# Graph attention layer, one core: the chunk end on VectorE and ScalarE, TensorE's program without loops, ScalarE's compares two steps ahead

## The reference

```python
# x: [8192, 128], adj: [8192, 8192] of 0 and 1, W: [128, 128], a_l, a_r: [4, 32]
mask = (adj + eye(8192)) > 0
Wh = (x @ W.T).reshape(8192, 4, 32)
l = einsum('nhd,hd->nh', Wh, a_l);  r = einsum('nhd,hd->nh', Wh, a_r)
e = l[:, :, None] + r.T[None, :, :]
e = where(e >= 0, e, 0.2 * e)
alpha = softmax(where(mask[:, None, :], e, -inf), axis=2)
out = elu(einsum('nhm,mhd->nhd', alpha, Wh).reshape(8192, 128))
y = layernorm(x + out)            # over the last axis, eps 1e-5
```

## Time and profile before

| | |
|---|---|
| median of 3 runs | 1956.38 us (1952.86 to 1957.16) |
| the profiled execution | 1956.05 us, span 1954.3 us |
| mean granted TensorE clock | 0.946 of 2.4 GHz |
| busy: TensorE matmul, VectorE, ScalarE, GpSimd | 86%, 95%, 87%, 12% |
| DMA | 418.06 MB, mean 214 GB/s |

### The profile page before, as it was taken

One profiled execution on the slowest core, in us unless ns is written; L12 is line 12 of the kernel. 1 busy time (PEld: TensorE's weight loads), 2 busy tenths in 40 slices (PEclk: granted clock), 3 DMA queues, 4 the chain that ended last, 5 costly groups with the idle time before them and its releaser, 6 DMA issues.

```text
span 1954.3 us, 83257 instructions
## 1 busy us (share of the span) xinstructions
PE 1676.7 (86%) x37063; PEld 1650.0 (84%) x37063; DVE 1850.1 (95%) x2056; ACT 1696.2 (87%) x1791; POOL 228.2 (12%) x106
## 2 busy tenths in 40 slices
PE   5188899798978999788988989889898889989894
PEld 5187799797978989788988989789897889989894
DVE  6699999999999999999999999999999999999995
ACT  3599899798988999798989989789897899979892
POOL 1000100401022010211004010220102110040103
PEclk8599999999999999999999999899998999999997
DMA  7899576676666767666766767567675657665221
GB/s 230 313 328 341 194 257 225 202 228 229 209 200 218 255 210 238 202 212 211 236 220 207 236 220 232 193 205 255 207 236 181 227 190 255 230 200 170 60 68 28
DMA packets 240287, 418.06 MB, mean 214 GB/s; under 512 B 14400, under 2 KB 104896, under 8 KB 238016
## 3 DMA queue, kind: packets, MB, share of 16 engines
q1 hardware_dynamic: 240064, 414.83, 64.6%
HBM read 397.48 MB, written 17.30 MB: 212 GB/s over the span
## 4 chain that ended last, share of the span: by engine, by line
ACT 44%; DVE 22%; PE 18%; issue 9%; DMA 5%; POOL 1%; SPq 0%; DVEq 0%; ACTq 0%; POOLq 0%
ACT bmask L446 40%; PE psum L335 15%; DVE bmask L591 7%; DVE bmask L603 5%; DVE cmask L609 5%; ACT acache L414 3%; DMA abuf<-in_adj_dram 3%; DVE acc L615 2%; DMA vring<-v_scratch 2%; PE trp L315 1%; PE psum L280 1%; DMA v_scratch<-vt 1%; DVE st L657 1%; PE psum L289 0%; DVE acache L539 0%
## 5 line engine op out<-in xcount | busy, mean ns | idle before, releaser
L446 ACT ACTIVATE bmask<-lrow,rtab 128x1024 fp8e4<-128x1024 f32 x1450 | 1540.7, 1149 | 11.5 <-PE psum L335 11.5
L335 PE MATMUL psum<-vring,bmask 128*128 128x99 bf16 x16384 | 843.0, 210 | 96.1 <-DVE bmask L603 48.1
L335 PE MATMUL psum<-vring,cmask 128*128 128x99 bf16 x16384 | 844.6, 211 | 89.1 <-DVE cmask L609 80.4
L335 PEld LDWEIGHTS psum<-vring,bmask 128*128 128x128 fp8e4 x16384 | 780.5, 99 | 107.8 <-issue 99.0
L335 PEld LDWEIGHTS psum<-vring,cmask 128*128 128x128 fp8e4 x16384 | 778.5, 99 | 100.5 <-issue 83.4
L603 DVE TENSOR_TENSOR bmask<-bmask,acache 128x1024 int32<-128x1024 int32 x512 | 632.2, 1235 | 41.3 <-ACT bmask L446 32.3
L609 DVE TENSOR_TENSOR cmask<-acache,bmask 128x1024 int32<-128x1024 int32 x512 | 654.7, 1279 | 11.8 <-PE psum L335 11.7
L591 DVE TENSOR_SCALAR bmask<-lrow,rtab 128x1024 fp8e4<-128x1024 f32 x598 | 500.0, 848 | 0.0
L414 ACT CAST acache<-trp 128x512 int32<-128x512 f32 x256 | 148.5, 580 | 167.3 <-PE trp L315 167.0
L720 POOL TENSOR_TENSOR late<-acc,wgt 128x1024 f32<-128x1024 f32 x16 | 45.0, 2810 | 1493.8 <-DVE wgt L645 1493.8
L315 PE MATMUL trp<-pack,abuf 128*128 128x32 bf16 x4096 | 144.1, 177 | 53.7 <-ACT acache L414 32.0
(11 more groups left out here) (60 smaller groups left out, 258.5 us busy)
## 6 DMA issues: line engine op xcount, KB each, us to landing
abuf<-in_adj_dram SPq DMA_DIRECT2D x256, 1024.0 KB, 8.0
vring<-v_scratch SPq DMA_DIRECT2D x512, 198.0 KB, 3.4
lrow<-l_scratch SPq DMA_DIRECT2D x16, 1024.0 KB, 10.8
v_scratch<-vt SPq DMA_DIRECT2D x16, 792.0 KB, 9.5
bmask<-in_x_dram SPq DMA_DIRECT2D x16, 256.0 KB, 2.9
late<-in_x_dram SPq DMA_DIRECT2D x32, 128.0 KB, 4.8
out_dram<-late SPq DMA_DIRECT2D x32, 128.0 KB, 6.1
l_scratch<-cmask SPq DMA_DIRECT2D x1, 128.0 KB, 3.7
```

The costliest lines, as they stand in the source:

```text
L335: return nc.tensor.matmul(psum[:, bank, at * S3:(at + 1) * S3], mask[:, i, j * P:(j + 1) * P], vring[:, slot, i, col:col + S3], start=open ...
L446: last = nc.scalar.activation(bmask[:, q % 4, h, i], lrow[:, p, h], ACT.Relu, bias=rtab[:, t, H + hh:H + hh + 1], scale=BIG, saturate=False)
```

## The change

- GpSimd's `weigh_sums`, `residual` and `normalise` go. It keeps two operations of 128x8 per chunk: variance + eps and the power.
- VectorE takes the multiplication by the weights in step 2 (128x1024), the sum of the branches and the minimum (128x512 each) in step 3. Once per chunk it makes `zz` = max(value, 0) + x in one operation in step 5 and adds exp - 1 in step 6 (before: 9). The statistics are in step 7 (before: 10), and `mean_part` (128x8) in step 9.
- ScalarE takes the exponential in step 4 (before: 6), and the normalisation itself: eight activations of 128x128 with a scale and a bias per row, two in each of the steps 11 to 14. The result lies in `em` and no longer in `pm`.
- ScalarE's iteration q now does compare(q + 2), and then the same evacuation. VectorE's compares stay one step ahead.
- TensorE's program is written out for all 512 steps: no loops, no registers, no `settle`. Its matmuls and their order are the same.

```diff
--- before.py
+++ after.py
@@ -109,7 +109,7 @@
         pm = late[:, 0:ITEMS * DK].rearrange("p (i d) -> p i d", d=DK)
         ov, mn, em, zz, xr = (late[:, ITEMS * DK + i * SUB * D:ITEMS * DK + (i + 1) * SUB * D].rearrange("p (j d) -> p j d", d=D)
                               for i in range(5))
-        yout = pm.rearrange("p i d -> p (i d)").rearrange("p (j d) -> p j d", d=D)
+        yout = em
         VF = G * 2 * HP * E
         WB = NT * HP * E
         whole = acache.rearrange("p t n -> p (t n)").bitcast(fp32)
...
@@ -204,14 +197,14 @@
                 return rows[c * CI:(c + 1) * CI, :].rearrange("(j s w) d -> s w j d", s=4, w=P // 4)[s]
 
             def load_xr(c):
-                wait(sp, y_ready, c)
+                wait(sp, z_done, c)
                 if c == 0:
                     sp.wait_ge(v_lo, NP * NG)
                 for s in range(4):
                     sp.dma_start(xr[s::4], as_bytes(x, c, s)).then_inc(xr_in, 16)
 
             def store_y(c):
-                sp.wait_ge(y_ready, c + 1)
+                sp.wait_ge(y_ready, SUB * (c + 1))
                 for s in range(4):
                     sp.dma_start(as_bytes(out, c, s), yout[s::4]).then_inc(y_stored, 16)
 
...
@@ -300,98 +290,55 @@
                 last = nc.tensor.transpose(psum[:, BANKS - 2, a * P:(a + 1) * P], l_t[:, a], identf[:, :])
             last.then_inc(l_back, 1)
 
-            def turn_pair(base, m, u):
-
-                buf = m // 2 % 2
-                if m % 2 == 0:
-                    pe.wait_ge(a_loaded[buf], 8 * base + 32 * u + 32 * (m // 4) + 32)
-                wait(pe, evac_done, base + m + 4 * u)
-                if not (isinstance(base, int) and isinstance(u, int)):
-                    settle()
+            def turn_pair(r):
+
+                buf = r // 2 % 2
+                if r % 2 == 0:
+                    pe.wait_ge(a_loaded[buf], 32 * (r // 4 + 1))
+                wait(pe, evac_done, r)
                 for i in range(2):
-                    at = (2 * m + i) % JB
+                    at = (2 * r + i) % JB
                     for j in range(SUB):
                         block_hi = abuf[:, buf, j, at * P:(at + 1) * P].bitcast(bf16)[:, 1::2]
                         last = nc.tensor.matmul(trp[:, i, j * P // 4:(j + 1) * P // 4], block_hi, pack[:, :], start=True, stop=True)
                 last.then_inc(tr_done, 1)
 
-            def step(c, p, u, k, first=False, turned=None):
-
-                slot, cslot = k % 4, k % 2
-                q = (c * NP + p) * STEPS + 8 * u + k
+            def step(q):
+                c, p, s = WHERE[q]
                 w = c * NP + p
-
-                def opens(bank):
-                    wait(pe, bank_free, BANKS * (w - 1) + bank + 1)
-                    if not isinstance(c, int):
-                        settle()
 
                 def product(mask, item, i, h, b, j):
                     bank, at = item // PB, item % PB
-                    opening = first and i == 0 and at == 0
+                    opening = s == 0 and i == 0 and at == 0
                     if opening:
-                        opens(bank)
+                        wait(pe, bank_free, BANKS * (w - 1) + bank + 1)
                     col = (h * 2 + b) * S3
                     return nc.tensor.matmul(psum[:, bank, at * S3:(at + 1) * S3], mask[:, i, j * P:(j + 1) * P],
-                                            vring[:, slot, i, col:col + S3], start=opening, stop=True, skip_group_check=True)
-
-                pe.wait_ge(v_in[slot], 16 * ((c * NP + p) * (STEPS // 4) + 2 * u + k // 4 + 1))
+                                            vring[:, q % 4, i, col:col + S3], start=opening, stop=True, skip_group_check=True)
+
+                pe.wait_ge(v_in[q % 4], 16 * (q // 4 + 1))
                 pe.wait_ge(b_ready, q + 1)
-                if not isinstance(q, int):
-                    settle()
                 for i in range(2):
                     for h in range(HP):
                         for j in range(SUB):
-                            last = product(bmask[:, slot, h], h * SUB + j, i, h, 0, j)
+                            last = product(bmask[:, q % 4, h], h * SUB + j, i, h, 0, j)
                 last.then_inc(half_done, 1)
-                if turned:
-                    turn_pair(*turned)
+                for r in TURNED[q]:
+                    turn_pair(r)
                 pe.wait_ge(c_ready, q + 1)
-                if not isinstance(q, int):
-                    settle()
                 for i in range(2):
                     for h in range(HP):
                         for j in range(SUB):
-                            last = product(cmask[:, cslot, h], (HP + h) * SUB + j, i, h, 1, j)
+                            last = product(cmask[:, q % 2, h], (HP + h) * SUB + j, i, h, 1, j)
                 last.then_inc(mm_done, 1)
...
-            def one_pass(c, p):
-
-                base = c * STEPS + p * STEPS // 2 + LEAD - LEAD % 4
-                eight(c, p, 0, True, base, SECOND, 0)
-                with pe.Fori(1, 4) as u:
-                    eight(c, p, u, False, base, SECOND, u)
 
             pe.wait_ge(pack_made, 1)
             for r in range(AHEAD):
-                turn_pair(0, r, 0)
+                turn_pair(r)
...
-            with pe.Fori(1, NC - 1) as c:
-                one_pass(c, 0)
-                one_pass(c, 1)
...
+            for q in range(Q):
+                step(q)
 
 
         @block.scalar
...
@@ -448,19 +395,27 @@
                 last.then_inc(cmp_act, 1)
 
             def elu_exp(w):
-                p = w % NP
-                act.wait_ge(mn_ready, w + 1)
-                nc.scalar.activation(em[:, :, p * HP * DK:(p + 1) * HP * DK], mn[:, :, p * HP * DK:(p + 1) * HP * DK],
-                                     ACT.Exp).then_inc(em_ready, 1)
+                c, p = w // NP, w % NP
+                mine = slice(p * HP * DK, (p + 1) * HP * DK)
+                act.wait_ge(mn_done, w + 1)
+                wait(act, y_stored, 4 * 16 * c)
+                nc.scalar.activation(em[:, :, mine], mn[:, :, mine], ACT.Exp).then_inc(em_done, 1)
+
+            def normalise(c, subs):
+                act.wait_ge(nmr_done, c + 1)
+                for j in subs:
+                    nc.scalar.activation(yout[:, j], zz[:, j], ACT.Identity, bias=nmr[:, j:j + 1],
+                                         scale=vrs[:, j:j + 1]).then_inc(y_ready, 1)
 
             act.wait_ge(um_done, 1)
             for b in range(2):
                 nc.scalar.activation(uu[:, :, b], um[:, b], ACT.Exp).then_inc(uu_done, 1)
             compare(0)
+            compare(1)
             for q in range(Q):
                 c, p, s = WHERE[q]
-                if q + 1 < Q:
-                    compare(q + 1)
+                if q + 2 < Q:
+                    compare(q + 2)
                 if q > 0:
                     for n in TURNED[q - 1]:
                         evacuate(n)
...
@@ -468,9 +423,12 @@
                     highest(NG + s // EVERY_STEPS)
                 if q < STEPS and s % EVERY_STEPS == 3:
                     middle(NG + s // EVERY_STEPS)
-                if s == 6 and q > STEPS:
+                if s == 4 and q > STEPS:
                     elu_exp(c * NP + p - 1)
+                if c > 0 and p == 0 and s in (11, 12, 13, 14):
+                    normalise(c - 1, (2 * s - 22, 2 * s - 21))
             elu_exp(NC * NP - 1)
+            normalise(NC - 1, range(SUB))
 
 
         @block.vector
...
@@ -618,8 +576,6 @@
 
             def take_first_sums(w):
                 dve.wait_ge(half_done, STEPS * (w + 1))
-                if w > 0:
-                    dve.wait_ge(pool_step, POOL_STEPS * ((w - 1) // 2) + 1 + 2 * ((w - 1) % 2))
                 add_parts(range(FIRST_BANKS))
 
             def take_last_sums(w):
...
+            def weigh_sums(w):
+                dve.wait_ge(dn_step, 4 * w + 4)
+                nc.vector.tensor_tensor(pm[:, :], acc[:, :, 0:DK], wgt.rearrange("p (i o) -> p i o", o=1).to_broadcast([P, ITEMS, DK]),
+                                        ALU.mult).then_inc(pm_done, 1)
+
+            def add_halves(w):
+                p = w % NP
+                mine = slice(p * HP * DK, (p + 1) * HP * DK)
+                p2 = pm.rearrange("p (b h j) d -> p b h j d", h=HP, b=2)
+                dve.wait_ge(pm_done, w + 1)
+                nc.vector.tensor_tensor(ov[:, :, mine].rearrange("p j (h d) -> p h j d", h=HP), p2[:, 0], p2[:, 1],
+                                        ALU.add).then_inc(ov_done, 1)
+                dve.wait_ge(ov_done, w + 1)
+                nc.vector.tensor_scalar(mn[:, :, mine], ov[:, :, mine], 0.0, None, ALU.min).then_inc(mn_done, 1)
+
+            def residual(c):
+                dve.wait_ge(ov_done, NP * (c + 1))
+                dve.wait_ge(xr_in, 4 * 16 * (c + 1))
+                wait(dve, y_ready, SUB * c)
```

(51 more changed lines are left out.)

76 lines of the change are left out of this document (8 added, 68 removed).

## The result

The changed kernel takes **1859.58 us** (median of 4 runs, 1858.71 to 1860.64), beside 1956.77 us for the kernel before on the same chip: a ratio of 0.9508, 95% interval 0.9491 to 0.9524. That is 97 us less. The forecast was 74 less. The profiled execution took 1858.71 us, with a span of 1856.8.

What follows compares the result with a forecast made beforehand. Three engines were nearly level, with VectorE late at the chunk end, slowed by GpSimd. From 1956 us: -91 GpSimd's work, +42 VectorE's new work, -17 ScalarE's lead, 0 TensorE's program, -8 the end, giving 1882; own range 1870 to 1897, whole 1858 to 1912.

Steps and rivals of the forecast that it cites:

- part 2: VectorE's new chunk-end work (weights, sum, minimum, zz, mean_part), with no cover: +42 us, bounds 38 and 52.
- part 3: ScalarE's compares two steps ahead shorten VectorE's waits for ScalarE: -17 us, bounds 0 and -32.
- Part 1: GpSimd's chunk-end work goes, so VectorE's compares and masks beside it are no longer slowed: -91 us.
- The rule that a saturated VectorE may shed work: Rival: long VectorE compares have another cause than GpSimd, so lost time does not come back: 1990 us, chance 0.02.
- the 22 that I took: VectorE's waits for ScalarE: 22 of the 29.6 us taken back through ScalarE's longer lead.
- The 5 that I had given back: Deduction of 5 us from the lead's gain, for TensorE being late next and ScalarE's new activations.
- part 4: TensorE's program written out, the chunk loop's branch being covered at the pass border: 0 us, bounds -10 and +11.
- The ring: Limit on ScalarE's lead: compare(q + 2) waits until step q - 2 is through TensorE; no separate size.
- The gaps in the middle of groups: TensorE's issue gaps between matmuls, 10.8 us in 17 places; at most some 11 us more from fetching every step.
- Part 5: After the last pass, from the weights to the store: 19.3 us becomes 11.3, -8 us.
- the first: Rival: ScalarE's lead lasts and TensorE keeps up: 1867 us, or 1858 with cheap new VectorE work; chance 0.22.
- the third rival: TensorE is starved of instructions at packet borders, some 340 packets, 40 in a pair of passes: 1970 us, chance 0.04.

Runs made afterwards that it cites:

- a_poolop: Changed kernel plus one GpSimd operation of 128x1024 per pass on a tile of its own, needed by nobody: 1886.51 us, ratio 0.9671.
- a_loops: Changed kernel with the earlier kernel's TensorE block back (Fori loops, registers, settle): 1877.69 us, ratio 0.9615.
- a_ring5: Changed kernel with five slots in place of four for the masks of branch 0, compares waiting for a step one further back: 1853.42 us.
- b_straight: Kernel before with TensorE's program written out and nothing else: 1951.79 us beside 1950.86, ratio 1.0008.
- a_nolead: Changed kernel with ScalarE's compares one step ahead again in place of two: 1890.14 us, ratio 0.9681.

## Why the prediction was right, and where it was not

The direction was right and the time lies in the whole range, 1858 to 1912, but only just, and outside my own range, 1870 to 1897. That it lies inside is luck as well: the low edge does not follow from my bounds. 1867 with 38 in place of 42 for part 2 is 1863, not 1858, and 1859.58 is below it.

The windows place the 97.5 us by which the span is shorter:

| | us |
|---|---|
| VectorE's busy time, passes 1 to 15 | -65.0 |
| VectorE's idle time, passes 1 to 15 | -26.0 |
| before pass 1 | -1.5 |
| after pass 15 | -5.0 |

Parts 1 and 2 stood for the first line, with -49, part 3 for the second, with -17. By the terms of the sum:

- **Part 1, -91: the right mechanism, 8 us too small.** 99.3 us came back. I had taken L591's undisturbed time from its busy sum, 500.0 - 598 x 0.748. But busy is the time in which at least one is under way, and pairs of compares overlap. The mean is the right number: 598 x (0.848 - 0.748) = 59.8, not 52.7. a_poolop shows the cause by itself. The two small GpSimd operations were indeed free: L549's mean is 0.747. With 8 us more here, parts 1 and 2 would give -57; the other 8 of the -65.0 are in none of my terms, and no run says where they come from.
- **Part 2, +42: right.** 1.22, 0.68, 0.43 and 1.22 us measured, for 1.22, 0.68, 0.40 and 1.22 taken. The rule that a saturated VectorE may shed work, even to GpSimd (the Trainium skill, Perfetto Trace Analysis, Optimizing Scalar/DVE Operations), would have meant 1990 us. The run decides against it here: VectorE with more work is busy 60 us less. The same section's reservation, that moves between these two might not help because they share a port, agrees with a_poolop; that it is the port, no run here shows.
- **Part 3, -17: too small.** VectorE's idle time in passes 1 to 14 fell by 25.3 us (39.9 to 14.6). Its waits for ScalarE fell by 21.7 (29.6 to 7.9), the 22 that I took. The 5 that I had given back, for TensorE being late next and for the activations, were not lost. TensorE was not late: VectorE's waits for it at mask_c are 11.0 us, as before (11.7), and none of them is in these passes. The activations cost more than I took, 0.487 us each for 0.25, and do not show in VectorE's waits. But the part has its -25.3 only with part 4's loops gone: with them (a_loops) the idle time is 31.2, down by 8.7. The ring was the limit of the lead, as said, and costs 6.5 us (a_ring5).
- **Part 4, 0: the step that failed.** "It stands at the pass border, where TensorE waits for VectorE's reductions anyway" came out for the kernel before (b_straight, 1.0008), and was false of the kernel that the other parts make. The cover was not the reductions, which end 1.2 us before TensorE resumes, but VectorE's delay beside GpSimd in the steps behind, which part 1 removes, and ScalarE's lateness, which part 3 removes: 5.8 and 4.7 us of waits with one of them alone, 14.2 with both. With the loops kept, the time is 1877.69 us, 73 us under its own kernel before; without them it is 18 us less by the times, 21 by the ratios. I had named the cover wrongly and not asked which of my own terms takes it away. I had also left out that TensorE runs at half its clock behind the stall. The gaps in the middle of groups did not grow with 292 packets, as I feared, but fell from 10.8 to 6.3 us. So what the Trainium skill says of fetching (Runtime: NRT & Kernel Launch, Instruction fetch mechanics), straight code mostly hidden and a stall for a taken branch that leaves the window, agrees with these runs: 6.3 us in 13 gaps are left, and the far branch costs 6.2 us and more. That the stall is the fetching, no row says. I should have leant on the section more.
- **Part 5, -8: nearly.** It was 6.6 us (19.3 to 12.7), since the eight activations take 3.18 us and not 2.0.

That a_loops comes out at the forecast is luck too: in its passes 1 to 14 VectorE's busy time fell by 61.4 us, for my -49 of parts 1 and 2, and its idle time by 8.7, for my -17.

Of the rivals, the first (lead lasts, TensorE keeps up, 1858 to 1867; it had 0.22) names what TensorE and ScalarE did, and the time lies in its range. But it does not account for the time: it changes part 3, to -32, and the idle time fell by 25 to 26; most of the distance from 1882 is in the busy time. What spoke against it, 3.06 us a step for TensorE against VectorE's 3.05, did not bite: TensorE is idle 13.8 us in each pair of passes. Of the third rival's fear, 292 packets came and not 340, and no gap over 1.0 us in passes 1 to 14.

The lead is worth 30 us by the times and 34 by the ratios (a_nolead), and removes 29 us of waits for ScalarE. The difference is within the intervals.

## What to carry to other kernels

A stall that costs nothing is hidden by something. Name what hides it and check whether another part of the same change takes that away; here a branch of 6.2 us five times was free until VectorE became quick and ScalarE got ahead, and then cost some 20 us. And an engine that does little can cost much: GpSimd, busy 12% of the span, held up VectorE by 99 us, and giving that work to the busiest engine made this one less busy.

## What the runs showed of the hardware

- Branches back over eight steps took up to 0.24 us and did not interrupt the matmuls; the one back over a pair of passes took 6.2 us in the median in the kernel before and 6.6 in a_loops, and TensorE stood still all that time. Behind it TensorE was granted 0.50, the lower of its two levels (1.2 GHz), for 2.8 to 3.3 us, and 32 matmuls took 2.83 us for 1.59. The row of a_loops (min/median/max ns):

```profile
L379 PEldq COMPARE_BRANCH  x6: 76/6602/6845, 546.5 to 1642.9; - x6
```

- The GpSimd operations on 128x8 did not hold VectorE up. The power takes 4.3 us in the steps and 1.6 in the empty end, and VectorE's compares beside it keep 0.75 us: the longest of the 598 in the changed kernel is 757 ns. One of 128x1024 holds a compare up for 1.6 us.
- An activation of 128x128 with scale and bias from SBUF takes 487 ns and one follows the other some 0.385 us later (eight in 3.18 us), while 128x512 without them takes 617 to 630.
